# A selective-state mixer whose result is kept with channels on the partitions, its decays read back from DRAM one chunk at a time

## The chip, the cores and the metric
The program runs on one core of a Trainium2 chip. The metric is the device time of one execution in microseconds (us): median of several runs.

## The reference, cut to what matters
Two layers. Layer 0 is a gated state-space mixer and an FFN, both on the same input; layer 1 is attention and a mixture of experts. Only the mixer's part is changed. It works on 2 sequences of 1024 tokens, width 256, with 64 heads of 64 channels in 8 groups (8 heads share one B and one C of 128 states):

```python
proj = einsum('bld,pd->blp', hidden_states, W_in)      # gate, x, B, C, dt
hbc  = silu(conv4(hbc) + conv_b)                       # causal, 4 taps, by channel
dt   = softplus(dt + dt_bias); Abar = dt * -exp(A_log)
scores  = einsum('bclhn,bcshn->bhcls', C_c, B_c)
Y_diag  = einsum('bhcls,bcshp->bclhp', scores * Lmat, x * dt)
states  = einsum('bcshn,bhcs,bcshp->bchpn', B_c, decay_states, x * dt)
Y_off   = einsum('bclhn,bchpn,bhcl->bclhp', C_c, prev_states, exp(A_cs))
Y = Y_diag + Y_off + D * x
g = Y * silu(gate)
out = (g * rsqrt(mean(g*g over the group) + EPS) * norm_weight) @ W_out.T
```

`A_cs` is the running sum of `Abar` inside a chunk, `Lmat` the lower triangle of exp of its differences. The reference cuts chunks of 32 tokens, the kernel of 128; the result does not depend on it.

## The kernel before, in words
The program is a row of stages: `prelude` (layernorm, layer 0's FFN, and the decays for all heads), `mixer`, a short sum, then layer 1. In `mixer` the time goes slot by slot: 128 chunks (8 groups of heads x 2 sequences x 8 chunks of 128 tokens), one slot each, after five slots that only fill. Each engine has its own program, written out in order by `for c in SLOTS`; semaphores tie them together. An engine does its instructions strictly in that order, so where an instruction stands decides what waits behind it. In slot `c`, chunk `c` is prepared, chunk `p = c - 1` is computed, and chunk `e = c - 2` is added to the result.

- **Blocks.** The projection of x, B and C is made in blocks of 128 channels x 384, 388 or 260 tokens, 18 for each group and sequence, so 2 or 3 blocks a slot (nine in four slots). Of each block TensorE does six passes (`fill`, the helper lines L75 to L77) into one of two PSUM banks `pp`; ScalarE starts the convolution (`init`, L966), VectorE adds three taps (`taps`, L1043), ScalarE takes a tanh (`squash`, L972) and VectorE finishes the silu (`finish`, L1050). For the last block of a slot, `squash` and `finish` come first in the next slot.
- **Preparing chunk c.** TensorE transposes x (L911) and B (L917), makes the scores (L918), and the decay exponents of 8 heads in two halves (`decays`, L872) through one PSUM bank `pd`. ScalarE copies x and B out (L993, L996) and takes exp of both halves (L1002, L1007). VectorE multiplies with the scores (L1093, 128x1024). GpSimd makes x times dt (L829), the same with the decay to the chunk's end (L832), and D times x (L834).
- **Computing chunk p, tokens on the partitions.** TensorE: C times the state carried in, 512 channels wide (L883), and 8 products of a head's 128x128 scores as weights with its 64 channels (L890). VectorE scales the first by exp(A_cs) (L1057), GpSimd adds D times x (L822), VectorE adds the two (`y`, L1068). The gate's projection is six passes of 512 columns (helper lines, into `pgt`), ScalarE's tanh (L989), VectorE's silu (L1073) and product (L1076). ScalarE squares and sums over the channels (L1012), GpSimd makes the rsqrt (L844, L846). TensorE transposes `y` (L949), ScalarE copies it out as `gt` (L981), and four products with `wo` (L941) and one VectorE instruction (L1103) add it to the result.
- **The state.** L928 on TensorE, L1085 or L1089 on VectorE, the decay on GpSimd (L839). The first chunk of a sequence has no state carried in, the last makes none.
- **Weights.** SP loads a group's `w_raw` and `wo_raw` two slots into the group before it; GpSimd splits them in nine pieces, one a slot (L799, L809, L812).

A float32 matmul is two passes in the trace (512 columns: L883 x2 in one group); the projections are three passes of rounded parts.

## Time and profile before

| | us |
|---|---|
| median of 3 runs | 2651.09 (2649.43 to 2652.48) |
| the profiled execution, its own time | 2650.09 |
| its span | 2648.4 |
| mixer, of the span | about 242 to 1612 |
| TensorE busy | 2365.0 (89%) |
| VectorE busy | 2069.6 (78%) |
| ScalarE, GpSimd busy | 1169.7, 1157.6 (44% each) |

The page's busy line says how much of the span an engine worked; what limits a stage has to be read in a stretch of that stage. "Idle before" is the time in which an engine stood still ahead of the instructions of a group, with the instruction that ended it. PEclk is the granted TensorE clock, 1.0 for 2.4 GHz.

### The profile page before, as it was taken

The numbers are of one execution on the slowest core, as the hardware profiler recorded it, in microseconds if no ns is written. First come the engines' busy times: TensorE is split into PE (matmuls) and PEld (weight loads), VectorE is DVE, ScalarE is ACT, GpSimd is POOL, SyncE is SP. The second block draws the span as 40 slices with busy tenths as digits, with TensorE's granted clock in tenths as the row PEclk, the third lists the DMA queues.
The fourth block names the chain that finished last, engine by engine and source line by source line (L and its number), as shares of the span: only waits on it lengthen the run. The fifth ranks groups of instructions, "written<-read, shape, count | busy, mean of one in ns | idle before, by whom it ended". The sixth has DMA issues, their size and how long they took to land. (4 is left out here: it accounts for less than half of the span.)

```text
span 2648.4 us, 41294 instructions
## 1 busy us (share of the span) xinstructions
PE 2365.0 (89%) x14084; PEld 1847.5 (70%) x14084; DVE 2069.6 (78%) x3420; ACT 1169.7 (44%) x2311; POOL 1157.6 (44%) x1249
## 2 busy tenths in 40 slices
...
PEclk9996899999999999999999997599999998699996
...
DMA packets 74320, 81.68 MB, mean 31 GB/s; under 512 B 21504, under 2 KB 57696, under 8 KB 72864
## 3 DMA queue, kind: packets, MB, share of 16 engines
...
## 5 line engine op out<-in xcount | busy, mean ns | idle before, releaser
L1043 DVE SCALAR_TENSOR_TENSOR mix_cv<-mix_pp,mix_cw,mix_cv 128x384 f32<-128x384 f32 (+4 forms) x864 | 493.0, 571 | 25.3 <-ACT mix_cv L966 4.5
L890 PEld LDWEIGHTS mix_pyd<-mix_xdt,mix_lm 128*128 128x128 f32 x2048 | 249.1, 193 | 56.7 <-issue 53.1
L966 ACT ACTIVATE mix_cv<-mix_pp,mix_cb,mix_cw 128x384 f32<-128x384 f32 (+1 forms) x288 | 182.1, 632 | 211.5 <-PE mix_pp L77 211.5
L75 PE MATMUL mix_pp<-l0in_XH,mix_wx_lo 128*128 128x384 f32 (+2 forms) x576 | 238.5, 414 | 39.3 <-DVE mix_ss L1032 23.3
L829 POOL TENSOR_TENSOR mix_xdt<-mix_xtok,l_dt 128x512 f32<-128x512 f32 x128 | 133.5, 1043 | 279.2 <-ACT mix_xtok L993 279.2
L1202 POOL TENSOR_TENSOR ffn_hl<-ffn_h,ffn_hh 128x512 fp32r<-128x512 f32 x112 | 144.3, 1288 | 250.5 <-ACT ffn_hh L1260 250.5
L941 PE MATMUL mix_pgt<-mix_wo,mix_gt 128*128 128x256 f32 x1024 | 244.9, 382 | 2.9 <-issue 2.2
L890 PE MATMUL mix_pyd<-mix_xdt,mix_lm 128*128 128x64 f32 x2048 | 244.4, 273 | 2.5 <-DVE mix_lm L1093 2.5
L822 POOL TENSOR_TENSOR mix_t<-mix_t,mix_xd 128x512 f32<-128x512 f32 x112 | 144.4, 1289 | 219.5 <-DVE mix_t L1057 136.9
L1725 DVE TENSOR_REDUCE att_tops<-att_psc 128x1 f32<-128x512 f32 (+3 forms) x384 | 190.0, 550 | 55.5 <-PE att_psc L1673 32.4
L941 PEld LDWEIGHTS mix_pgt<-mix_wo,mix_gt 128*128 128x128 f32 x1024 | 184.1, 190 | 31.2 <-issue 9.2
L972 ACT ACTIVATE mix_pp<-mix_cv 128x384 f32<-128x384 f32 (+1 forms) x288 | 133.0, 462 | 161.6 <-DVE mix_cv L1043 158.3
L1749 ACT ACTIVATE att_pr<-att_pst 128x1024 f32<-128x1024 f32 (+7 forms) x256 | 156.5, 657 | 103.6 <-PE att_pst L1690 73.7
L77 PE MATMUL mix_pp<-l0in_XH,mix_wx_hi 128*128 128x384 f32 (+2 forms) x576 | 188.0, 326 | 0.0
L76 PE MATMUL mix_pp<-l0in_XL,mix_wx_hi 128*128 128x384 f32 (+2 forms) x576 | 187.9, 326 | 0.0
L1276 DVE SCALAR_TENSOR_TENSOR ffn_h<-ffn_th,ffn_pg 128x512 f32<-128x512 f32 x112 | 77.0, 687 | 137.4 <-ACT ffn_th L1255 137.4
L1260 ACT ACTIVATE ffn_hh<-ffn_h 128x512 fp32r<-128x512 f32 x112 | 71.2, 636 | 249.0 <-DVE ffn_h L1283 249.0
L1093 DVE TENSOR_TENSOR mix_lm<-mix_lm,mix_pmisc 128x1024 f32<-128x1024 f32 x128 | 156.1, 1219 | 23.0 <-ACT mix_lm L1007 21.3
L75 PEld LDWEIGHTS mix_pp<-l0in_XH,mix_wx_lo 128*128 128x128 f32 x576 | 111.6, 194 | 88.0 <-DVE mix_cv L1050 38.3
L1068 DVE TENSOR_TENSOR mix_y<-mix_pyd,mix_t 128x512 f32<-128x512 f32 x112 | 77.5, 692 | 111.2 <-POOL mix_t L822 111.2
L1050 DVE SCALAR_TENSOR_TENSOR mix_cv<-mix_pp,mix_cv 128x384 f32<-128x384 f32 (+1 forms) x288 | 145.7, 506 | 9.3 <-ACT mix_pp L972 9.3
L75 PE MATMUL ffn_po<-ffn_dh,ffn_hl 128*128 128x256 f32 x448 | 145.0, 324 | 4.2 <-DVE l_F L1290 4.2
...
## 6 DMA issues: line engine op xcount, KB each, us to landing
...
mix_ll<-cs SPq DMA_DIRECT2D x384, 4.0 KB
mix_wo_raw<-in_w_out SPq DMA_DIRECT2D x8, 512.0 KB, 6.5
...
```

Source lines behind the costliest of these rows:

```text
L75: pe.matmul(out, l_lo, r_hi, start=start, stop=False)
L76: pe.matmul(out, l_hi, r_lo, start=False, stop=False)
L77: return pe.matmul(out, l_hi, r_hi, start=False, stop=stop)
L822: pool.tensor_tensor(t1[p % 2][:, :], t1[p % 2][:, :], xd[p % 2][:, :], ALU.add).then_inc(t1x_done, 1)
L890: last = pe.matmul(pyd[:, h * HP:(h + 1) * HP], lm[p % 2][:, h, :], xdt[p % 2][:, h * HP:(h + 1) * HP], start=True, stop=True)
L941: last = pe.matmul(pgt[:, 0:D], gt[e % 2][:, k * P:(k + 1) * P], wo[:, e // 16 % 2, k, :], start=k == 0, stop=k == NX - 1)
L966: act.activation(conv_tile(k), pp[k % 2][:, halo:cols], ACT.Identity, bias=cb[:, it // 2, ct:ct + 1], scale=cw[:, it // 2, ct, 3:4]).then_ ...
L1043: last = dve.scalar_tensor_tensor(out, of, cw[:, g, ct, 3 - d:4 - d], out, ALU.mult, ALU.add)
L1050: dve.scalar_tensor_tensor(c, pp[k % 2][:, 0:cols - halo], 1.0, c, ALU.add, ALU.mult).then_inc(conv_done, 1)
L1093: dve.tensor_tensor(lm[c % 2][:, :, :], lm[c % 2][:, :, :], pmisc[:, N0:N0 + Q].unsqueeze(1).to_broadcast([P, GH, Q]), ALU.mult).then_inc( ...
L1725: dve.tensor_reduce(tops[o][:, col:col + 1], psc[PLACE[n, g] % RING][:, 0:end - c], AX.X, ALU.max).then_inc(mx_done, 1)
L1749: act.activation(pr[m % 2][:, AT[k]:AT[k + 1]], pst[k % 2][:, 0:1024 - k * P], ACT.Exp).then_inc(ex_done, 1)
```

## The change
The mixer's result is now kept with the channels on the partitions.

- **Off-diagonal and diagonal parts.** For each head one product with the carried state as weights (128x64) and `ce` = C times exp(A_cs) as data (128 columns), and one with x times dt as weights (128x64) and the scores as data, both into the same place in `py` (L918, L920). Even heads write partitions 0 to 63, odd heads 64 to 127. 16 products of 128 columns take the place of one of 512 and eight of 64 columns. The transposes of `y`, their copy, L1057 and L822 are gone.
- **ce.** The table exp(A_cs) goes to DRAM in the prelude (two transfers), laid out by chunk, so that 8 heads x 128 tokens are one run of 4 KB. SP reads it for each chunk to all 128 partitions (512 KB, 112 times, L798), behind a wait for the product that last read the buffer; GpSimd multiplies it with C (128x1024, L842).
- **D times x** is now four 128x128 ScalarE copies with a scale for each channel (L1035).
- **Gate.** Twelve passes of 256 columns for two chunks' tokens and half of the channels, one slot earlier (`gate(c + 1)`), ahead of the second half of the decays. Its tanh (L1026) stands between the two exps on ScalarE; VectorE writes its silu (L1102) to `sg` in SBUF.
- **Sum of squares.** ScalarE squares without a sum (L1008), GpSimd adds four blocks in two instructions (L846, L849), TensorE sums over the partitions with a column of ones (L959); ScalarE copies the sum out (L1002), GpSimd does one power (L838).
- **Order.** On TensorE, `decays(c, 1)` stood behind the slot's last block and now stands ahead of the middle block and the state; the product with `wo` (L964) is done for `p` instead of `e`. On VectorE the addition to the result (L1086) moves from the slot's end to near its start.
- **Loads.** SP loads a group's weights behind waits for the last group's projections and products; `wo` is loaded in place. There is one slot less at the end.

```diff
@@ TensorE
-                        pe.matmul(pyos[:, :], cv[:, CT_C, cols_of(p)], carry[:, :], start=True, stop=True).then_inc(yo_done, 1)
...
-                        for h in range(GH):
-                            last = pe.matmul(pyd[:, h * HP:(h + 1) * HP], lm[p % 2][:, h, :],
-                                             xdt[p % 2][:, h * HP:(h + 1) * HP], start=True, stop=True)
+                        for k in range(NX):
+                            if p % CPS:
+                                for h in (2 * k, 2 * k + 1):
+                                    pe.matmul(head_out(h), carry[:, h * HP:(h + 1) * HP], ce[p % 2][:, h, :], start=True, stop=False)
+                            for h in (2 * k, 2 * k + 1):
+                                last = pe.matmul(head_out(h), xdt[p % 2][:, h * HP:(h + 1) * HP], lm[p % 2][:, h, :],
+                                                 start=p % CPS == 0, stop=True)
...
                         decays(c, 0)
+                    if 0 <= c + 1 < NC:
+                        gate(c + 1)
+                    if live:
+                        decays(c, 1)
                     if len(ks) > 2:
                         fill(ks[1])
...
                         fill(ks[-1])
-                    if live:
-                        decays(c, 1)
...
+                        pe.matmul(px[:, D:D + 1], zs[:, :], one[:, :], start=True, stop=True)
@@ ScalarE
                         act.activation(lm[o][:, 0:4, :].rearrange("p h l -> p (h l)"), pd[:, :], ACT.Exp).then_inc(l_done, 1)
+                    if 0 <= c + 1 < NC:
+                        act.wait_ge(gate_done, c + 2)
+                        wait(act, w_done, c + 1)
+                        act.activation(tg[:, :], pgt[:, :], ACT.Tanh, scale=0.5).then_inc(tg_done, 1)
+                    if live:
+                        act.wait_ge(d_done, 2 * c + 2)
+                        act.activation(lm[o][:, 4:8, :].rearrange("p h l -> p (h l)"), pd[:, :], ACT.Exp).then_inc(l_done, 1)
@@ VectorE
-                        dve.tensor_tensor(by_head(t1[o]), by_head(pyos), heads(TE1, p), ALU.mult).then_inc(t1_done, 1)
                     if len(fills(c - 1)) > 1:
                         finish(fills(c - 1)[-1])
+                    if 0 <= e < NC:
+                        dve.wait_ge(op_done, e + 1)
+                        dve.wait_ge(rs_done, e + 1)
+                        row = ACC[:, e // CPS % 2 * CPS + e % CPS, :]
+                        dve.scalar_tensor_tensor(row, px[:, 0:D], rs[e % 2][:, 0:1], row, ALU.mult, ALU.add).then_inc(acc_done, 1)
...
                     if ks:
                         taps(ks[0])
-                    if 0 <= p < NC:
-                        dve.wait_ge(tg_done, p + 1)
-                        dve.scalar_tensor_tensor(pgt[:, :], tg[:, :], 1.0, pgt[:, :], ALU.add, ALU.mult).then_inc(w_done, 1)
+                    if 0 <= c + 1 < NC:
+                        u = c + 1
+                        dve.wait_ge(tg_done, u + 1)
+                        dve.scalar_tensor_tensor(sg[:, u // 2 % 2, u % 2 * 2:u % 2 * 2 + 2, :].rearrange("p k l -> p (k l)"),
+                                                 tg[:, :], 1.0, pgt[:, :], ALU.add, ALU.mult).then_inc(w_done, 1)
                     if ks:
                         finish(ks[0])
@@ SP
+                    if j:
+                        wait(sp, yd_done, c - 1)
+                        sp.dma_start(ce[c % 2][:, :, :], ecs_d[b * CPS + j, g * GH:(g + 1) * GH, :].partition_broadcast(P)).then_inc(ecs_in[c % 2], 16)
```

ScalarE's program in the middle of the mixer, one slot of two blocks, before:

```order
L981 ACTIVATE mix_gt<-mix_pxt 128x512
L972 ACTIVATE mix_pp<-mix_cv 128x384
L966 ACTIVATE mix_cv<-mix_pp,mix_cb,mix_cw 128x384
L989 ACTIVATE mix_tg<-mix_pgt 128x512
L993 ACTIVATE mix_xtok<-mix_pxt 128x512
L996 ACTIVATE mix_btok<-mix_pmisc 128x128
L972 ACTIVATE mix_pp<-mix_cv 128x384
L1002 ACTIVATE mix_lm<-mix_pd 128x512
L1007 ACTIVATE mix_lm<-mix_pd 128x512
L1012 ACTIVATE mix_junk,mix_ss<-mix_y 128x512
L966 ACTIVATE mix_cv<-mix_pp,mix_cb,mix_cw 128x384
```

and now (L989 is now the tanh of a block, L983 its start, L1026 the gate's tanh):

```order
L989 ACTIVATE mix_pp<-mix_cv 128x384
L1002 ACTIVATE mix_ss<-mix_px,mix_eps_sum 128x1
L983 ACTIVATE mix_cv<-mix_pp,mix_cb,mix_cw 128x384
L1008 ACTIVATE mix_zsq<-mix_z 128x512
L1013 ACTIVATE mix_xtok<-mix_px 128x512
L1016 ACTIVATE mix_btok<-mix_pmisc 128x128
L989 ACTIVATE mix_pp<-mix_cv 128x384
L1022 ACTIVATE mix_lm<-mix_pd 128x512
L1026 ACTIVATE mix_tg<-mix_pgt 128x512
L1029 ACTIVATE mix_lm<-mix_pd 128x512
L1035 ACTIVATE mix_xd<-mix_cv,mix_dsk 128x128 x4
L983 ACTIVATE mix_cv<-mix_pp,mix_cb,mix_cw 128x384
```

The gate's tanh has moved from ahead of the first block's tanh to behind it and behind the first exp.

VectorE's program there, from the finish of the last slot's block on, before:

```order
L1057 TENSOR_TENSOR mix_t<-mix_pyos,l_exp_cs 128x512
L1050 SCALAR_TENSOR_TENSOR mix_cv<-mix_pp,mix_cv 128x384
L1068 TENSOR_TENSOR mix_y<-mix_pyd,mix_t 128x512
L1043 SCALAR_TENSOR_TENSOR mix_cv<-mix_pp,mix_cw,mix_cv 128x384 x3
L1073 SCALAR_TENSOR_TENSOR mix_pgt<-mix_tg,mix_pgt 128x512
L1076 TENSOR_TENSOR mix_y<-mix_y,mix_pgt 128x512
L1050 SCALAR_TENSOR_TENSOR mix_cv<-mix_pp,mix_cv 128x384
```

and now (L1069 the taps, L1076 the finish of a block, L1102 the gate's silu):

```order
L1076 SCALAR_TENSOR_TENSOR mix_cv<-mix_pp,mix_cv 128x384
L1086 SCALAR_TENSOR_TENSOR main_X<-mix_px,mix_rs,main_X 128x256
L1093 TENSOR_TENSOR mix_z<-mix_py,mix_xd 128x512
L1095 TENSOR_TENSOR mix_z<-mix_z,mix_sg 128x512
L1069 SCALAR_TENSOR_TENSOR mix_cv<-mix_pp,mix_cw,mix_cv 128x384 x3
L1102 SCALAR_TENSOR_TENSOR mix_sg<-mix_tg,mix_pgt 128x512
L1076 SCALAR_TENSOR_TENSOR mix_cv<-mix_pp,mix_cv 128x384
L1109 TENSOR_TENSOR mix_lm<-mix_lm,mix_pmisc 128x1024
```

The addition to the result has come between the finish and the chunk's sum, and L1057 is gone.

TensorE's program there, around the slot's start, now (L77 is the block's last pass, L964 the product with `wo`):

```order
L77 MATMUL mix_pp<-l0in_XH,mix_w_hi 128x384
L959 MATMUL mix_px<-mix_one,mix_zs 128x1
L964 MATMUL mix_px<-mix_wo,mix_z 128x256 x4
L918 MATMUL mix_py<-mix_ce,mix_carry 64x128 x2
L920 MATMUL mix_py<-mix_lm,mix_xdt 64x128 x2
```

The pair L918, L920 comes four times. Before, the second half of the decays stood between L77 and the product with `wo`, which the transposes of `y`, the 512 wide L883 and the eight L890 followed.

## Rows read from the trace of the kernel before
**Rows 1.** The page: busy time by engine, and the granted clock in 40 slices.
```profile
PE 2365.0 (89%) x14084; PEld 1847.5 (70%) x14084; DVE 2069.6 (78%) x3420; ACT 1169.7 (44%) x2311; POOL 1157.6 (44%) x1249
...
PEclk9996899999999999999999997599999998699996
```
**Rows 2.** Busy time in one stretch of the mixer, 700 to 1500 us.
```profile
700.00:1500.00 800.00, 787.28 (x4739) 655.64 (x4738) 705.74 (x1204) 444.58 (x955) 476.93 (x537) 1.00 0.04 12
```
**Rows 3.** Groups of VectorE instructions, 700 to 1500 us: xcount | busy us, mean ns | idle before.
```profile
L1043 DVE SCALAR_TENSOR_TENSOR mix_cv<-mix_pp,mix_cw,mix_cv 128x256 f32<-128x256 f32 (+2 forms) x516 | 293.3, 568 | 12.2
L1093 DVE TENSOR_TENSOR mix_lm<-mix_lm,mix_pmisc 128x1024 f32<-128x1024 f32 x77 | 93.9, 1219 | 13.6 <-ACT mix_lm L1007 12.6
...
L1068 DVE TENSOR_TENSOR mix_y<-mix_pyd,mix_t 128x512 f32<-128x512 f32 x66 | 45.7, 692 | 64.5 <-POOL mix_t L822 64.5
L1057 DVE TENSOR_TENSOR mix_t<-mix_pyos,l_exp_cs 128x512 f32<-128x512 f32 x67 | 45.6, 681 | 0.0
```
**Rows 4.** Timeline of the mixer, TensorE: start us, us, engine line op.
```profile
1001.61 1.89 PE L941 MATMUL mix_pgt<-mix_wo,mix_gt 128*128 128x256 f32 x8
...
1003.34 0.60 PE L949 MATMUL mix_pxt<-all_ident,mix_y 128*128 128x128 f32 x4
...
1003.78 1.02 PE L883 MATMUL mix_pyos<-mix_carry,mix_cv 128*128 128x512 f32 x2
...
1004.64 1.89 PE L890 MATMUL mix_pyd<-mix_xdt,mix_lm 128*128 128x64 f32 x16
...
1006.34 0.42 PE L75 MATMUL mix_pp<-l0in_XH,mix_wx_lo 128*128 128x384 f32 x1
...
1009.85 1.02 PE L928 MATMUL mix_pyos<-mix_xdtd,mix_btok 128*128 128x512 f32 x2
...
1011.77 0.39 PE L872 MATMUL mix_pd<-mix_rl,mix_ll 96*128 96x256 bf16 x2
```
**Rows 5.** Timeline of the attention: TensorE, outputs on four partition ranges.
```profile
2402.68 1.05 PE L1705 MATMUL att_po<-att_pr,l_V 128*17 128x512 f32 x8
2403.67 0.39 PE L1673 MATMUL att_psc<-att_ks,att_qs 96*128 96x512 bf16 x1
```
**Rows 6.** Timeline of the mixer: ScalarE and VectorE.
```profile
1007.67 0.67 ACT L966 ACTIVATE mix_cv<-mix_pp,mix_cb,mix_cw 128x384 f32<-128x384 f32 x1 [1.61 <-PE mix_pp L77]
...
1008.53 1.91 DVE L1043 SCALAR_TENSOR_TENSOR mix_cv<-mix_pp,mix_cw,mix_cv 128x383 f32<-128x383 f32 x3
...
1010.47 0.50 ACT L972 ACTIVATE mix_pp<-mix_cv 128x384 f32<-128x384 f32 x1 [0.16 <-DVE mix_cv L1043]
...
1010.90 0.58 ACT L1002 ACTIVATE mix_lm<-mix_pd 128x512 f32<-128x512 f32 x1
...
1016.24 0.68 DVE L1057 TENSOR_TENSOR mix_t<-mix_pyos,l_exp_cs 128x512 f32<-128x512 f32 x1
...
1016.84 0.55 DVE L1050 SCALAR_TENSOR_TENSOR mix_cv<-mix_pp,mix_cv 128x384 f32<-128x384 f32 x1
```
**Rows 7.** Timeline of the mixer's first blocks: VectorE.
```profile
245.01 0.56 DVE L1050 SCALAR_TENSOR_TENSOR mix_cv<-mix_pp,mix_cv 128x384 f32<-128x384 f32 x1 [0.56 <-ACT mix_pp L972]
```
**Rows 8.** Timeline of the mixer's last chunks: VectorE.
```profile
1593.62 1.22 DVE L1093 TENSOR_TENSOR mix_lm<-mix_lm,mix_pmisc 128x1024 f32<-128x1024 f32 x1 [0.21 <-ACT mix_lm L1007]
...
1602.25 1.22 DVE L1093 TENSOR_TENSOR mix_lm<-mix_lm,mix_pmisc 128x1024 f32<-128x1024 f32 x1 [0.21 <-ACT mix_lm L1007]
```
**Rows 9.** Groups of ScalarE instructions, 700 to 1500 us.
```profile
L989 ACT ACTIVATE mix_tg<-mix_pgt 128x512 f32<-128x512 f32 x76 | 45.4, 597 | 57.2 <-PE mix_pgt L77 57.2
...
L1012 ACT ACTIVATION_READ_ACCUMULATOR mix_junk<-mix_y 128x1 f32 x77 | 14.9, 193 | 0.0
```
**Rows 10.** Groups of GpSimd instructions, 700 to 1500 us.
```profile
L846 POOL TENSOR_TENSOR mix_rs<-mix_rs,mix_half 128x1 f32<-128x1 f32 x77 | 42.3, 549 | 6.0
...
L799 POOL TENSOR_TENSOR mix_wo<-mix_wo_raw,mix_nw 128x1024 f32<-128x1024 f32 x5 | 9.5, 1893 | 0.0
```
**Rows 11.** DMA issues: bytes, median us from issue to landing.
```profile
mix_wo_raw<-in_w_out SPq DMA_DIRECT2D x8, 512.0 KB, 6.5
```

335 lines of the change are left out of this document (166 added, 169 removed).

## The prediction
> **What bounds the kernel now.** I read the page first. TensorE is busy for 89% of the span, no other engine for more than 78% [rows 1]. That share is a mean over stages, so I looked at a stretch inside the mixer, the only stage whose work changes: of 800 us TensorE is busy for 787.3 and VectorE for 705.7, and the granted clock is 1.00, the 2.4 GHz level [rows 2]. TensorE paces the mixer; VectorE follows closely.
>
> How long a slot is: the stretch holds 76.5 slots (L1093 appears 77 times [rows 3], its neighbours 76), so a slot is 800 / 76.5 = 10.46 us. VectorE works 705.7 / 76.5 = 9.22 us of it and stands still for 1.23. The groups of VectorE say where: 64.5 us ahead of L1068 (it waits for GpSimd's sum, which ends when VectorE isn't needed yet), 13.6 ahead of L1093, 12.2 ahead of the taps [rows 3]; what is left of the 94.3 us is 4.0. So the slack of VectorE is 1.23 us a slot. A busy engine in second place with that little slack is what decides here: if the change gives VectorE new waits of more than it takes work away, VectorE paces the mixer in TensorE's place.
>
> **The change on TensorE.** From the start of one instruction to the start of the next [rows 4]: L883 0.86 us (1003.78 to 1004.64), the eight L890 1.70, the transposes of `y` 0.44 (four of 128 columns, 0.11 each). The new group is 16 float32 products of 128 columns, thus 32 passes of 0.107: 3.42 us if they go one after the other, 1.71 if the two heads of a pair, on different partitions of the output, go side by side. The trace of before has such a case: L1705 writes four partition ranges, and eight passes of 512 columns, 0.43 each by L883 x2, are followed by the next matmul after 0.99 us [rows 5], not after 3.4. They ran four abreast, with 0.13 us lost at the switch. I take side by side: 1.71 us and two switches, 0.26. The Trainium skill speaks against it: "TensorE: Matmul & The Clock Gate", Part 3, The mechanism, says that a weight load overlaps running matmuls only where the row groups differ, and both heads here use all 128 rows. By that rule this group would come near the 3.42 us; the row of L1705, whose loads also use 128 rows, disagrees. That row has 17 columns of weights and ours 64, so the rule stays as a rival. The sum of squares is two passes of one column behind a full weight load, 0.21 by the transposes' pace. The gate's twelve passes of 256 columns carry as many columns as the six of 512: nothing, or 0.03.
> Net on TensorE: -0.86 - 1.70 - 0.44 + 1.71 + 0.26 + 0.21 + 0.03 = -0.79 us a slot, to some 9.7.
>
> **The change on VectorE, work.** L1057 goes: 0.60 us from its start to the next [rows 6], in 7 of 8 chunks, -0.52. The other instructions keep their sizes: the chunk's sum and product, the gate's silu, L1109, the state, the addition. Reading `sg` from SBUF instead of PSUM I count at nothing. Work: 9.22 - 0.52 = 8.70 us.
>
> **The change on VectorE, waits.** These come from where the instructions now stand, and the order shows them.
> (a) Behind the first block's taps VectorE's next instruction is the gate's silu (L1102). It needs the gate's tanh, which ScalarE does behind the first block's tanh and behind the first exp. The block's tanh needs the taps. So after each first block VectorE stands still for three ScalarE instructions: 0.02 + 0.46 (mean of the forms; 0.50 for 384 columns) - 0.06 + 0.59 - 0.07 + 0.60 + 0.03 = 1.57 us. The steps are rows: taps end at 1010.44, the tanh starts at 1010.47, the exp at 1010.90, 0.07 before the tanh ends [rows 6]; the gate's tanh takes 0.597 [rows 9]. Before, the gate's tanh stood ahead of all this and the silu found it done.
> (b) The last block's taps are followed at once by its finish, which needs ScalarE's tanh. In the first slots, where nothing lies between, this costs 0.56 us each time [rows 7]; 0.51 over the forms. Before, L1057 or the addition filled it.
> (c) The addition to the result has moved behind that finish. It needs GpSimd's power (0.549 [rows 10]), that needs ScalarE's copy of the sum (about 0.19, as the one-column read [rows 9]), and that comes behind the same tanh: 0.19 + 0.08 + 0.55 + 0.03 - 0.06 = 0.79 from the tanh's end, against 0.54 for the finish, so 0.25 more.
> (d) The other small waits, 12.2 + 4.0 us in 76.5 slots, stay: 0.21. The waits for L822 and ahead of L1093 go, since (a) covers them.
> VectorE's round: 8.70 + 1.57 + 0.51 + 0.25 + 0.21 = 11.24 us, against 10.46: +0.78 us a slot. This is a closed ring, as VectorE's own order closes it, and TensorE at 9.7 fits inside.
>
> **Does something else end later?** The ring through TensorE: the second half of the decays needs the first exp, and behind it in order stand the state (0.85), the block (1.07), the sum of squares, the product with `wo` (1.73), the new group and the next first block (1.07), whose taps release the tanh and the exp again. 0.22 + 0.85 + 1.07 + 0.21 + 1.73 + 1.97 + 1.07 = 7.1 on TensorE, then 0.2 to the block's start on ScalarE, 0.67, taps 1.92, and 1.1 for tanh and exp [rows 4, 6]: 11.0 us for two blocks of 384 columns. VectorE's ring over the same blocks is 11.1: the mean of 11.24 has 2.25 blocks of 0.568 x 3 + 0.50 = 2.2 us [rows 3], thus 5.0 us of block work, where two of 384 columns have 1.91 x 2 + 0.55 x 2 = 4.9. So TensorE waits for the exp in every slot and hides inside VectorE's ring with only 0.1 us to spare there; slots of three blocks have more, since the third adds 2.2 us to VectorE's ring and 1.07 to TensorE's.
> GpSimd works 476.9 / 76.5 = 6.2 us of a slot now [rows 2]. It gets L842 (1.9, the size of L799 [rows 10]) and two small sums, and loses L822, D times x and a small addition; even with nothing taken off for these it has 9 us of work in 11, and L842 has most of a slot's time. ScalarE works 444.6 / 76.5 = 5.8 us; it gets four copies of a quarter of L989's size (at most 0.6 each) and loses the transposed copy, and the four stand where it waits for the next block. Neither is on the path; an excess would show as a later xtok and then a later product. SP's transfer for `ce`: 512 KB, 6.5 us to landing for a transfer of that size behind a larger one [rows 11]. SP issues it when the product of two chunks before is done, 12 us before GpSimd's turn, so nothing waits; if that cover were gone, GpSimd and then the next slot's products would wait by the excess. The small decay tables queue behind it for at most those 6.5 us and are needed a slot later. The waits on other groups' weights are over when SP comes to them. The prelude's two transfers are issued while its products still run: nothing. I count `wo` in place at nothing.
>
> **The sum.** 123 slots carry blocks: 123 x 0.78 = +96 us. The last four have none and take 8.63 us now (L1093 at 1593.62 and 1602.25 [rows 8]); without taps only (c) is left there, and TensorE's saving counts: -0.5 each, -2 us. The slot less at the end is empty. Sum: +94 us on the profiled execution, 2650.1 to 2744; the median of the runs is 1 us above that execution, so **2745 us**.
>
> Bounds of this case: with (c) and (d) at nothing the ring is 10.78, +0.32 us a slot, +37 us: 2688. With the products only partly side by side (2.6 us instead of 1.71) TensorE's ring takes over at 11.9 less 0.3 for the shorter forms, or where memory traffic lengthens VectorE's instructions by 4% the ring is about as long: 11.6 to 11.7, +150 us at most: 2800; with both a little more, 2830.
>
> **Rivals.**
> 1. Faster. TensorE goes on to set the pace, as it does now. This needs VectorE's waits to stay below 10.46 - 8.70 = 1.76 us a slot, where I find 2.54; that is the point from which it decides. For it: TensorE was busy for 98.4% of the stretch [rows 2], and the change takes 0.79 us a slot from it. Against it: (a) and (b) alone are 2.08, and both follow from the order, not from estimates. The time: 128 x -0.79 = -101 us, 2550. It would need the gate's tanh to be ready when the taps end.
> 2. Much slower. The head pairs do not run side by side. TensorE's ring then has 3.42 for 1.71 and no switch: 12.4 for 384 columns, about 12.2 over the forms, +1.75 us x 123 = +215: 2866. For it: weights of 64 columns are not 17, and the skill's rule above. Against it: L1705 [rows 5].
> 3. The change does not do what it says: `ce` comes too late, and each slot waits for it. For this 512 KB would have to take 12 us, not 6.5 [rows 11]; priced at +1 to +3 us a slot it gives 2780 to 3030.
>
> **How the numbers follow.** VectorE's ring as told 0.81, rival 1 0.10, rival 2 0.06, rival 3 0.03. The forecast is the first case's. The range 2688 to 2830 is that case's own with its bounds, and leaves out about 2 in 10: the other three and a little of its edges. Within 0.2% (5 us, about what a measurement of this kernel can tell from no change) lies only a ring where the waits happen to cancel, 1.76 us: 0.02. Faster: 0.10. Slower: 0.88.
>
> **What would show it.** In the profile after: a slot of 11.2 us; idle ahead of the gate's silu (L1102) released by ScalarE's gate tanh (L1026), about 1.57 us a time, 190 us in all; idle ahead of the finish (L1076) about 0.5 and ahead of the addition (L1086) about 0.25; TensorE busy for some 87% of the mixer at a clock that stays at 1.00, and waiting at L896 for the exp; the pair L918, L920 in about 2 us for 32 passes. If L1102 finds its tanh done, the forecast is wrong in its main term; if the 32 passes take 3.4 us, rival 2 holds; if GpSimd's L842 waits for a DMA, rival 3.

## The result and the profile after

| | us |
|---|---|
| before, median of 4 runs | 2651.03 (2649.43 to 2652.48) |
| after, median of 4 runs | 2927.73 (2921.61 to 2929.92) |
| ratio | 1.104, interval 1.1025 to 1.106 |
| span of the profiled execution after | 2927.5 |

The change makes the kernel 277 us slower. The direction was forecast; the size was not: 2927.7 lies 98 us above the upper end of the range, 2830. The mixer now lasts from about 242 to about 1898 us.

The stretch of [rows 2], the same 800 us of the kernel after (the columns are those of [rows 2]: TensorE, its weight loads, VectorE, ScalarE, GpSimd, granted clock, DMA share, GB/s):

```profile
700.00:1500.00 800.00, 654.91 (x4916) 550.68 (x4915) 605.10 (x929) 413.79 (x965) 453.15 (x442) 0.93 0.13 45
```

The groups below appear 62 or 63 times, so the stretch holds some 62.4 slots of **12.8 us**, where 11.2 was forecast. VectorE works 605.1 / 62.4 = 9.70 us of a slot and stands still for 3.12; TensorE works 10.50 and no engine is busy for even 82% of the stretch. The granted clock is 0.93, a mean of spells at its two levels, where it was 1.00 before.

VectorE's groups after, same stretch, the answer to [rows 3] (count | busy us, mean ns | idle before):

```profile
L1069 DVE SCALAR_TENSOR_TENSOR mix_cv<-mix_pp,mix_cw,mix_cv 128x256 f32<-128x256 f32 (+4 forms) x421 | 240.1, 570 | 34.1 <-ACT mix_cv L983 22.7
L1095 DVE TENSOR_TENSOR mix_z<-mix_z,mix_sg 128x512 f32<-128x512 f32 x62 | 92.2, 1488 | 2.1
...
L1093 DVE TENSOR_TENSOR mix_z<-mix_py,mix_xd 128x512 f32<-128x512 f32 x63 | 42.9, 681 | 3.8 <-PE mix_py L920 3.7
L1102 DVE SCALAR_TENSOR_TENSOR mix_sg<-mix_tg,mix_pgt 128x512 f32<-128x512 f32 x62 | 42.6, 687 | 94.3 <-ACT mix_tg L1026 94.3
...
L1086 DVE SCALAR_TENSOR_TENSOR main_X<-mix_px,mix_rs,main_X 128x256 f32<-128x256 f32 x63 | 30.4, 483 | 27.1 <-POOL mix_rs L838 27.1
```

The wait that was the main term is there and has its forecast size: 94.3 / 62.4 = 1.51 us a slot ahead of L1102, 1.57 forecast, released by the gate's tanh. But the second row was not in the forecast: the product with `sg`, L1095, takes **1488 ns**, and the sum before it, L1093, of the same size, 681. The small waits (d), forecast at 0.21, are larger too: 34.1 / 62.4 = 0.55 us a slot ahead of the taps, L1069, alone. Then TensorE and GpSimd, groups of the same stretch:

```profile
L896 PE MATMUL mix_pd<-mix_rl,mix_ll 96*128 96x256 bf16 x248 | 53.0, 299 | 123.7 <-ACT mix_lm L1022 123.7
```
```profile
L842 POOL TENSOR_TENSOR mix_ce<-mix_ce,mix_cv 128x1024 f32<-128x1024 f32 x55 | 130.7, 2377 | 0.0
```

TensorE stands still 2.0 us a slot ahead of L896 for the first exp. L842 takes 2.38 us, not 1.9.

One slot of the timeline shows how these hang together. GpSimd and VectorE:

```profile
1009.45 2.38 POOL L842 TENSOR_TENSOR mix_ce<-mix_ce,mix_cv 128x1024 f32<-128x1024 f32 x1
```
```profile
1010.50 0.69 DVE L1093 TENSOR_TENSOR mix_z<-mix_py,mix_xd 128x512 f32<-128x512 f32 x1 [0.44 <-PE mix_py L920]
1011.22 1.15 DVE L1095 TENSOR_TENSOR mix_z<-mix_z,mix_sg 128x512 f32<-128x512 f32 x1
1012.29 1.51 DVE L1069 SCALAR_TENSOR_TENSOR mix_cv<-mix_pp,mix_cw,mix_cv 128x256 f32<-128x256 f32 x3
```

L1093 reads PSUM and SBUF and runs in 0.69 beside L842. L1095 reads two operands from SBUF. It starts while L842 is under way (to 1011.83) and ends at 1012.37, 0.54 after L842's end. The whole mixer shows the same: in all 111 slots in which the two overlap, L1095 ends 0.54 to 0.56 behind L842, whenever it started, and in the 17 slots without such an overlap (most of them slots that prepare a sequence's first chunk, which has no `ce` product) it takes 0.69. So at most some 0.15 of its 0.69 us of work was done while GpSimd's instruction ran. The Trainium skill, "SBUF — State Buffer", section "Who interferes with whom", has this rule: a VectorE instruction with two SBUF inputs contends with a GpSimd instruction that reads SBUF, and whichever starts first holds the shared ports to its end. The trace agrees, and the prediction had not weighed it.

TensorE in the slot before, with the idle time ahead of L896 in brackets, and in the slot after it:

```profile
1003.01 0.39 PE L896 MATMUL mix_pd<-mix_rl,mix_ll 96*128 96x256 bf16 x2 [1.96 <-ACT mix_lm L1022]
...
1004.41 0.42 PE L77 MATMUL mix_pp<-l0in_XH,mix_w_hi 128*128 128x260 f32 x1
...
1005.56 3.00 PE L964 MATMUL mix_px<-mix_wo,mix_z 128*128 128x256 f32 x8
...
1008.48 0.44 PE L918 MATMUL mix_py<-mix_ce,mix_carry 128*64 128x128 f32 x4
...
1010.38 0.39 PE L75 MATMUL mix_pp<-l0in_XH,mix_w_lo 128*128 128x260 f32 x1
...
1010.72 0.28 PE L77 MATMUL mix_pp<-l0in_XH,mix_w_hi 128*128 128x260 f32 x1
...
1014.79 0.39 PE L896 MATMUL mix_pd<-mix_rl,mix_ll 96*128 96x256 bf16 x2 [1.01 <-ACT mix_lm L1022]
...
1016.74 1.97 PE L964 MATMUL mix_px<-mix_wo,mix_z 128*128 128x256 f32 x8
```

and busy time and clock of that stretch:

```profile
996.00:1003.00 7.00, 3.63 (x29) 3.19 (x27) 5.03 (x8) 3.44 (x9) 4.47 (x5) 1.00 0.20 75
1003.00:1008.00 5.00, 4.99 (x19) 4.09 (x20) 4.11 (x7) 3.07 (x8) 3.86 (x4) 0.66 0.02 4
```

In the seven microseconds to 1003 TensorE was busy for 3.63; behind them the granted clock is 0.66 as a mean over 1003 to 1008. A pass of 260 columns takes 0.42 us there, and 0.28 in the next slot; the product with `wo` takes 3.00 us there and 1.97 in the next slot: part of the first is at 1.2 GHz, the second at 2.4. So, as it looks here, the long idle time is paid for a second time, in the work that follows it; run 10 tests this. The group L918, L920 lies from 1008.48 to 1010.38: 32 passes in **1.90 us**, where 1.97 was forecast for passes side by side.

### The profile page after: what moved, and what is told of

Read it like the earlier page. It is cut to its first block and busy times, and to the rows that moved or that the text cites. A ratio compares the mean times of both kernels' runs of the same rounds, so it can differ in the third digit from the quotient of the medians.

```text
span 2927.5 us, 45825 instructions
## 1 busy us (share of the span) xinstructions
PE 2371.3 (81%) x16164; PEld 1864.9 (64%) x16164; DVE 2121.9 (72%) x3308; ACT 1273.2 (43%) x2695; POOL 1275.9 (44%) x1250
## 5 line engine op out<-in xcount | busy, mean ns | idle before, releaser
L1069 DVE SCALAR_TENSOR_TENSOR mix_cv<-mix_pp,mix_cw,mix_cv 128x384 f32<-128x384 f32 (+4 forms) x864 | 492.4, 570 | 70.1 <-ACT mix_cv L983 46.6
L896 PE MATMUL mix_pd<-mix_rl,mix_ll 96*128 96x256 bf16 x512 | 108.8, 297 | 252.4 <-ACT mix_lm L1022 252.4
L75 PE MATMUL mix_pp<-l0in_XH,mix_w_lo 128*128 128x384 f32 (+2 forms) x576 | 272.7, 473 | 33.6 <-DVE mix_ss L1058 23.2
L983 ACT ACTIVATE mix_cv<-mix_pp,mix_cb,mix_cw 128x384 f32<-128x384 f32 (+1 forms) x288 | 181.7, 631 | 266.4 <-PE mix_pp L77 264.4
L989 ACT ACTIVATE mix_pp<-mix_cv 128x384 f32<-128x384 f32 (+1 forms) x288 | 132.1, 459 | 344.3 <-DVE mix_cv L1069 341.5
L964 PE MATMUL mix_px<-mix_wo,mix_z 128*128 128x256 f32 x1024 | 271.4, 411 | 0.0
L842 POOL TENSOR_TENSOR mix_ce<-mix_ce,mix_cv 128x1024 f32<-128x1024 f32 x112 | 266.2, 2377 | 0.0
L1102 DVE SCALAR_TENSOR_TENSOR mix_sg<-mix_tg,mix_pgt 128x512 f32<-128x512 f32 x128 | 88.0, 687 | 196.5 <-ACT mix_tg L1026 196.5
L838 POOL TENSOR_TENSOR mix_rs<-mix_ss,mix_half 128x1 f32<-128x1 f32 x128 | 70.2, 549 | 366.1 <-ACT mix_ss L1002 364.5
L896 PEld LDWEIGHTS mix_pd<-mix_rl,mix_ll 96*128 96x128 bf16 x512 | 40.9, 101 | 279.7 <-ACT mix_lm L1022 278.2
L964 PEld LDWEIGHTS mix_px<-mix_wo,mix_z 128*128 128x128 f32 x1024 | 199.0, 205 | 24.5
L76 PE MATMUL mix_pp<-l0in_XL,mix_w_hi 128*128 128x384 f32 (+2 forms) x576 | 201.9, 351 | 0.0
L77 PE MATMUL mix_pp<-l0in_XH,mix_w_hi 128*128 128x384 f32 (+2 forms) x576 | 201.1, 349 | 0.0
L1076 DVE SCALAR_TENSOR_TENSOR mix_cv<-mix_pp,mix_cv 128x384 f32<-128x384 f32 (+1 forms) x288 | 146.7, 509 | 71.0 <-ACT mix_pp L989 71.0
L920 PE MATMUL mix_py<-mix_lm,mix_xdt 128*64 128x128 f32 x2048 | 191.6, 273 | 1.3 <-DVE mix_lm L1109 1.3
L1095 DVE TENSOR_TENSOR mix_z<-mix_z,mix_sg 128x512 f32<-128x512 f32 x128 | 187.8, 1467 | 4.4
L75 PEld LDWEIGHTS mix_pp<-l0in_XH,mix_w_lo 128*128 128x128 f32 x576 | 125.0, 217 | 100.4 <-issue 50.9
L918 PE MATMUL mix_py<-mix_ce,mix_carry 128*64 128x128 f32 x1792 | 179.8, 279 | 0.0
```

Source lines behind the costliest of these rows:

```text
L75: pe.matmul(out, l_lo, r_hi, start=start, stop=False)
L76: pe.matmul(out, l_hi, r_lo, start=False, stop=False)
L77: return pe.matmul(out, l_hi, r_hi, start=False, stop=stop)
L842: pool.tensor_tensor(ce[o][:, :, :], ce[o][:, :, :], cv[:, CT_C, cols_of(c)].unsqueeze(1).to_broadcast([P, GH, Q]), ALU.mult).then_inc(ce_ ...
L918: pe.matmul(head_out(h), carry[:, h * HP:(h + 1) * HP], ce[p % 2][:, h, :], start=True, stop=False)
L920: last = pe.matmul(head_out(h), xdt[p % 2][:, h * HP:(h + 1) * HP], lm[p % 2][:, h, :], start=p % CPS == 0, stop=True)
```

## The experiments

A ring is a chain of work and waits that closes on itself once a slot; no slot is shorter than the longest ring. The theory behind the first four: the product with `sg`, held up by the `ce` product, and TensorE's clock are the parts that the forecast lacked; the waits (a) to (c) are near their forecast (1.51, 0.54 and 0.43 us a slot). The rivals: the transfers are to blame, or VectorE's wait (a) alone.

**1. The `ce` product behind x times dt on GpSimd.**

```diff
@@ GpSimd, behind the power (L838)
-                    if live and c % CPS:
...
-                        pool.tensor_tensor(ce[o][:, :, :], ce[o][:, :, :],
...
                            pool.tensor_tensor(by_head(xdtd[o]), by_head(xtok[o]), heads(TDTD, c), ALU.mult).then_inc(xdtd_done, 1)
+                    if live and c % CPS:
...
+                        pool.tensor_tensor(ce[o][:, :, :], ce[o][:, :, :],
```

> The changed kernel with one GpSimd instruction moved: the product that makes ce (L842) now stands behind the two products with dt, and no longer runs while VectorE multiplies z by the gate (L1095). Theory (the two share the way to SBUF): L1095 falls from 1.47 us to 0.69, and VectorE's ring is 0.78 us a slot shorter; 2830 us if that ring alone sets the slot, down to 2880 if the ring through TensorE takes over. Rival (L1095 is slow because both of its inputs lie in SBUF): it stays at 1.47 us and the time at 2928.

Measured: 2787.14 us, ratio 1.051 (1.049 to 1.053): 140.6 us less than after the change. The groups and the stretch of this run:

```profile
L1095 DVE TENSOR_TENSOR mix_z<-mix_z,mix_sg 128x512 f32<-128x512 f32 x68 | 47.1, 692 | 2.4
```
```profile
700.00:1500.00 800.00, 671.76 (x5380) 567.44 (x5378) 609.70 (x1023) 456.09 (x1068) 499.02 (x488) 1.00 0.15 51
```

The product is back at 692 ns and the clock at 1.00. The gain is larger than the 98 us expected of the product alone; the half-clock spells went too, and run 10 prices them by themselves at 52 us or more.

**2. The gate's tanh ahead of the first block's tanh on ScalarE**, nothing else.

```diff
@@ ScalarE
+                        act.activation(tg[:, :], pgt[:, :], ACT.Tanh, scale=0.5).then_inc(tg_done, 1)
                     if ks:
                         squash(ks[0])
...
                         act.activation(lm[o][:, 0:4, :].rearrange("p h l -> p (h l)"), pd[:, :], ACT.Exp).then_inc(l_done, 1)
...
-                        act.activation(tg[:, :], pgt[:, :], ACT.Tanh, scale=0.5).then_inc(tg_done, 1)
```

> The changed kernel with the gate's tanh moved on ScalarE ahead of the first block's tanh, where it stood before the change. Theory (VectorE's ring): the idle ahead of the gate's silu, 1.52 us a slot, goes; the ring through TensorE (second half of the decays behind the first exp) is then close to being the longer one: 2740 to 2790 us. Rival (TensorE's ring at the lowered clock sets the slot already): less than 40 us gained, 2890 or more, and the idle turns up ahead of another VectorE instruction.

Measured: 2936.83 us, ratio 1.108 (1.106 to 1.110), 9 us more than after. The expected 2740 to 2790 missed; the rival's number (less than 40 us gained) came true. The wait (a) is down from 94.3 to 14.5 us in the stretch, and the time is not: VectorE's groups of this run say where it went.

```profile
L1109 DVE TENSOR_TENSOR mix_lm<-mix_lm,mix_pmisc 128x1024 f32<-128x1024 f32 x62 | 75.7, 1221 | 60.4 <-ACT mix_lm L1029 60.4
...
L1102 DVE SCALAR_TENSOR_TENSOR mix_sg<-mix_tg,mix_pgt 128x512 f32<-128x512 f32 x62 | 42.6, 688 | 14.5 <-ACT mix_tg L1020 14.2
```

VectorE gets through the silu earlier and waits for the second exp instead; TensorE still waits 125.3 us in the stretch ahead of L896. Another ring was as long. But the long product and the half-clock spells are both still in this run, so run 3 is the cleaner test.

**3. Both moves together**: the two edits above, nothing else.

> Both moves of the two runs before. Theory: VectorE's ring would be 12.85 - 0.78 - 1.52 = 10.55 us, below the 11.0 us reckoned for TensorE's ring; TensorE's rules: 2700 to 2740 us, TensorE idle ahead of L896 still over 1 us a slot, VectorE idle ahead of the taps. Rival (TensorE's ring rules already): 2850 or more.

Measured: 2789.26 us, ratio 1.053 (1.051 to 1.055): the same as with the first alone, where 2700 to 2740 was expected. So the tanh's place is worth nothing while the `ce` product is out of the way as well. VectorE's wait ahead of L1102 fell from 105.2 us in the stretch (run 1) to 33.1, and 57.6 came up ahead of L1109, for the second exp. TensorE waits longer than in run 1 (89.4) for the first exp:

```profile
L896 PE MATMUL mix_pd<-mix_rl,mix_ll 96*128 96x256 bf16 x274 | 53.1, 275 | 106.9 <-ACT mix_lm L1026 106.9
```

**4. The table is not read from the fourth chunk on** (two numbers are read in its place; the `ce` product is then made from what lies in the buffer).

```diff
@@ SP
+                        if c < 3:
                             sp.dma_start(ce[c % 2][:, :, :], ecs_d[b * CPS + j, g * GH:(g + 1) * GH, :].partition_broadcast(P)).then_inc(ecs_in[c % 2], 16)
+                        else:
+                            sp.dma_start(ce[c % 2][:, 0, 0:2], ecs_d[b * CPS + j, g * GH, 0:2].partition_broadcast(P)).then_inc(ecs_in[c % 2], 16)
```

> The changed kernel with the table of decays read only for the first three chunks; for the others SP reads two numbers a partition, so ce and with it the carried state's part is wrong from then on. All waits stay. Theory: the 57 MB cost nothing, 2928 us within 6, L1095 and L842 as long as before. Rival (the transfers get in the way of VectorE, GpSimd or SP): 2900 or less, L842 nearer to 1.9 us and L1095 shorter.

Measured: 2931.84 us, ratio 1.106 (1.104 to 1.108). The DMA share of the stretch falls from 0.13 to 0.03, the product stays at 1475 ns, and the time stays within the 6 us expected (4 us more). The transfers cost nothing.

**5. The chunk's sum stays in PSUM**, so that the product reads one operand there; the `ce` product stays in its place. TensorE's next group, which writes the same place in PSUM, then has to wait for the product instead of the sum.

```diff
@@ VectorE
-                        dve.tensor_tensor(flat(z[p % 2]), py[:, :], flat(xd), ALU.add).then_inc(u_done, 1)
+                        dve.tensor_tensor(py[:, :], py[:, :], flat(xd), ALU.add).then_inc(u_done, 1)
...
-                        dve.tensor_tensor(z[p % 2][:, :, :], z[p % 2][:, :, :],
+                        dve.tensor_tensor(z[p % 2][:, :, :], py[:, :].rearrange("p (k l) -> p k l", k=NX),
@@ TensorE
-                        wait(pe, u_done, p)
+                        wait(pe, z_done, p)
```

> The changed kernel with one tile moved: the chunk's sum is written back to PSUM in place, so that the z product (L1095) reads one operand from PSUM and only sg from SBUF. GpSimd's ce product stays where it is. Theory A (two instructions whose operands all lie in SBUF, one on VectorE and one on GpSimd, hold each other up, which made L1095 1.49 us long and the ce product 2.38): L1095 falls to about 0.7 us, the ce product to about 1.9 to 2.1, the taps come 0.8 us earlier, and the time falls to about 2790, as in the run with the ce product moved. Theory B (the ce product's place on GpSimd delayed something else, a late xtok or xdt, and the long z product was only a symptom): L1095 gets shorter, but the time stays within 1% of 2928. Theory C (any two SBUF accesses of the two engines collide, however many operands): L1095 stays above 1.2 us.

Measured: 2770.26 us, ratio 1.044 (1.042 to 1.046), 157.5 us less than after. VectorE's and GpSimd's groups, the stretch, and one slot:

```profile
L1102 DVE SCALAR_TENSOR_TENSOR mix_sg<-mix_tg,mix_pgt 128x512 f32<-128x512 f32 x70 | 48.2, 689 | 106.5 <-ACT mix_tg L1026 106.5
L1095 DVE TENSOR_TENSOR mix_z<-mix_py,mix_sg 128x512 f32<-128x512 f32 x69 | 47.7, 692 | 2.3
...
L1086 DVE SCALAR_TENSOR_TENSOR main_X<-mix_px,mix_rs,main_X 128x256 f32<-128x256 f32 x70 | 33.9, 484 | 25.0 <-POOL mix_rs L838 25.0
```
```profile
L842 POOL TENSOR_TENSOR mix_ce<-mix_ce,mix_cv 128x1024 f32<-128x1024 f32 x61 | 145.3, 2381 | 0.0
```
```profile
700.00:1500.00 800.00, 676.87 (x5450) 574.07 (x5451) 616.84 (x1035) 460.06 (x1079) 506.42 (x494) 1.00 0.15 51
```
```profile
1018.48 2.37 POOL L842 TENSOR_TENSOR mix_ce<-mix_ce,mix_cv 128x1024 f32<-128x1024 f32 x1
...
1019.74 0.69 DVE L1095 TENSOR_TENSOR mix_z<-mix_py,mix_sg 128x512 f32<-128x512 f32 x1
```

L1095 still lies wholly inside L842, and takes 0.69 us. One operand's place decides: 1488 to 692 ns, with both instructions where they were. That settles theory A for VectorE, and rules out theory B (the time fell by 5%) and C. It was wrong for GpSimd: L842 takes 2381 ns here too, and 2383 in run 1, where it stands elsewhere, so 2.38 us is its own length.

**6. The same in the kernel before**: the gate's silu goes to a tile in SBUF, so that the product with it (L1076 before, 687 ns there) has two SBUF inputs.

```diff
@@ VectorE of the kernel before
-                        dve.scalar_tensor_tensor(pgt[:, :], tg[:, :], 1.0, pgt[:, :], ALU.add, ALU.mult)
+                        dve.scalar_tensor_tensor(sgx[:, :], tg[:, :], 1.0, pgt[:, :], ALU.add, ALU.mult)
...
-                        dve.tensor_tensor(y[o][:, :], y[o][:, :], pgt[:, :], ALU.mult)
+                        dve.tensor_tensor(y[o][:, :], y[o][:, :], sgx[:, :], ALU.mult)
```

> The kernel before with one tile moved: the gate's silu goes to a tile in SBUF, so that the product with it (L1077 here) has all operands in SBUF, as L1095 has after the change; it took 0.68 us with one operand in PSUM. Theory A: it grows where GpSimd works on full tiles at the same time (44% of the time there), so its mean comes to 0.8 to 1.1 us, with single ones near 1.5; VectorE has 1.23 us of slack a slot, so the time rises by at most 10 us (2651 to 2661). Rival: the length comes from something else in the changed kernel; then the product stays at 0.68 to 0.72 and the time at 2651.

Measured: 2694.97 us, ratio 1.0166 (1.0149 to 1.0182). The product and GpSimd's product with the decay in the kernel before, then VectorE's and GpSimd's groups of this run (the lines are one higher than before the edit):

```profile
L1076 DVE TENSOR_TENSOR mix_y<-mix_y,mix_pgt 128x512 f32<-128x512 f32 x76 | 52.2, 687 | 2.6
```
```profile
L832 POOL TENSOR_TENSOR mix_xdtd<-mix_xtok,l_dt_decay 128x512 f32<-128x512 f32 x67 | 69.9, 1043 | 0.0
```
```profile
L1077 DVE TENSOR_TENSOR mix_y<-mix_y,mix_sgx 128x512 f32<-128x512 f32 x74 | 85.1, 1150 | 2.6
...
L1069 DVE TENSOR_TENSOR mix_y<-mix_pyd,mix_t 128x512 f32<-128x512 f32 x64 | 44.3, 692 | 62.4 <-POOL mix_t L823 62.4
```
```profile
L833 POOL TENSOR_TENSOR mix_xdtd<-mix_xtok,l_dt_decay 128x512 f32<-128x512 f32 x64 | 87.0, 1359 | 0.0
```

The product grows from 687 to 1150 ns, as theory A says, and GpSimd's L833 from 1043 to a mean of 1359: a single one takes 1.04 us, or 1.49 where VectorE's product came first. This is the rule in both directions. The time was under-estimated, +44 us and not at most +10: VectorE's 0.84 us of slack a slot is still there ahead of L1069 (62.4 us), a wait that comes before the product and so did not take it up. The taps behind the product come later, and TensorE, idle for 12.7 us of the stretch before, is idle for 32.1. Of the product's 0.46 us a slot, 0.34 (44 us over 128 slots) reached the time. Slack ahead of the work that grows was of little use here.

**7. Both rings opened, the `ce` product late.** From run 3, moved on top: the second half of the decays back behind the slot's last block on TensorE, the second exp ahead of the last block's start and D times x behind it, the product with the scores behind the state on VectorE.

```diff
@@ TensorE
-                    if live:
-                        decays(c, 1)
                     if len(ks) > 2:
                         fill(ks[1])
...
                         fill(ks[-1])
+                    if live:
+                        decays(c, 1)
```

> The changed kernel with the ce product moved behind x times dt and its decayed form on GpSimd, the gate's tanh ahead of the first block's tanh on ScalarE, and beyond that: on TensorE the second half of the decays stands behind the slot's last block again, on ScalarE the second exp directly ahead of the last block's start with D times x behind that, and on VectorE the product with the scores behind the carried state, ahead of the last taps. Theory R (the ring that sets 11.65 us a slot in the run with the ce product moved goes through the wait of the second half of the decays for the first exp): the idle ahead of L896 nearly goes (under 0.3 us a slot from 1.3), the slot falls to 10.2 to 10.5 us and the time to 2600 to 2660. Rival (VectorE's own order is the bound by itself): the slot stays above 11.2 us and the time above 2740.

Measured: 2739.34 us, ratio 1.033 (1.031 to 1.035). Theory R missed. The slot (11.3 us) is the rival's and the time lies at its edge (above 2740), but the reason is not its own. The idle ahead of L896 went (106.9 to 4.7 us in the stretch), but a new one stands elsewhere: 61.9 us ahead of L918, 45.0 of it for the `ce` product, late since run 1's move.

**8. As 7, and the addition to the result ahead of the last block's finish** (ScalarE's copy of the sum ahead of that block's tanh).

```diff
@@ VectorE
+                        dve.scalar_tensor_tensor(row, px[:, 0:D], rs[e % 2][:, 0:1], row, ALU.mult, ALU.add).then_inc(acc_done, 1)
                     if len(fills(c - 1)) > 1:
                         finish(fills(c - 1)[-1])
...
-                        dve.scalar_tensor_tensor(row, px[:, 0:D], rs[e % 2][:, 0:1], row, ALU.mult, ALU.add).then_inc(acc_done, 1)
```

> The run before it, and ScalarE's copy of the sum of squares stands ahead of the last block's tanh, VectorE's addition to the result ahead of its finish. Theory: waits (b) and (c) of the prediction, 0.51 and 0.25 us a slot, are then filled by work that stands there already; if VectorE's round sets the slot by then, it falls by 0.4 to 0.75 us, to 9.7 to 10.0, and the time to 2560 to 2600, below both kernels. Rival: TensorE's round of 9.7 to 9.8 us of work and its own waits set the slot; then it falls by under 0.2 us, the time within 25 us of the run before it. Third way: the addition waits for the product with wo longer than the finish waited for the tanh, and the time rises.

Measured: 2718.05 us, ratio 1.026 (1.024 to 1.027): 21 us less, far above the 2560 to 2600 expected and inside the rival's 25 us. The wait ahead of the finish goes (3.7 us left), the addition waits instead. TensorE's and VectorE's groups:

```profile
L918 PE MATMUL mix_py<-mix_ce,mix_carry 128*64 128x128 f32 x1008 | 106.6, 277 | 71.6 <-POOL mix_ce L855 54.4 <-DVE mix_lm L1120 17.2
```
```profile
L1084 DVE SCALAR_TENSOR_TENSOR main_X<-mix_px,mix_rs,main_X 128x256 f32<-128x256 f32 x73 | 35.1, 481 | 89.1 <-POOL mix_rs L838 89.1
```

Most of both points at one cause, which run 9 tests: the `ce` product, 2.37 us here, stands late on GpSimd, and the power behind it.

**9. As 8, with the sum in PSUM (run 5) and the `ce` product back in its first place.** The edit is that of run 5 in place of that of run 1:

```diff
@@ GpSimd, behind the power again
+                        pool.tensor_tensor(ce[o][:, :, :], ce[o][:, :, :],
@@ VectorE
+                        dve.tensor_tensor(py[:, :], py[:, :], flat(xd), ALU.add).then_inc(u_done, 1)
```

> The order of e8_reordered_acc_first, with the chunk's sum in PSUM as in e5_sum_in_psum, so that the ce product can go back to its first place on GpSimd at no cost for VectorE. In e8 TensorE stood still 1.0 us a slot ahead of the group L918, 54.4 of 71.6 us of it for the ce product, and the addition waited 1.24 us a slot for GpSimd's power, which stood behind the ce product. Theory (these two waits are what the late place of the ce product costs): both fall below 0.4 us a slot, the slot from 11.1 to 10.2 to 10.4 us, the time to 2600 to 2650, below or at the kernel before. Rival: VectorE's round (8.9 us of work and its waits for the exps) sets the slot at 10.8 or more, and the time stays above 2680.

Measured: **2605.83 us**, ratio 0.983 (0.982 to 0.984), 1.7% faster than the kernel before and inside the 2600 to 2650 expected. The stretch:

```profile
700.00:1500.00 800.00, 758.80 (x6135) 644.05 (x6135) 698.37 (x1166) 508.19 (x1215) 559.54 (x549) 1.00 0.17 57
```

The stretch holds 78.5 slots of 10.2 us; TensorE works 758.8 / 78.5 = 9.67 us of each. The wait ahead of L918 is down from 71.6 to 27.6 us, none of it for the `ce` product, and that of the addition from 89.1 to 2.1.

**10. The kernel after, with more work for TensorE.** The gate's twelve passes are done twice, ahead of the place where TensorE waits.

```diff
@@ TensorE, gate
-                    for t in range(2):
+                    for t in (0, 1, 0, 1):
```

> The changed kernel, with the gate's twelve passes done twice over (the second time onto the same values, so the result is the same): 1.4 us more work for TensorE in each slot at full clock, put in the place where it stands still for 2.0 us a slot ahead of L896. Theory K (the half-clock spells are a cost of their own, brought on by that idle time): TensorE does not stand still long enough for its clock to fall, the granted clock of the stretch 700 to 1500 comes back to 1.00 and the time falls by 20 to 60 us, to 2870 to 2905, in spite of more work. Rival L (the half-clock spells only fill idle time and cost nothing): the time stays at 2928 or rises, by up to 50 us, as the gate's tanh comes 1.4 us later.

Measured: 2875.32 us, ratio 1.085 (1.083 to 1.086): 52 us **less** than after, with 1.4 us more work in every slot (twelve passes that start 0.12 us apart), as theory K said. Its stretch, L896, and VectorE's taps:

```profile
700.00:1500.00 800.00, 723.38 (x5853) 627.85 (x5853) 628.35 (x966) 429.81 (x1008) 468.59 (x457) 1.00 0.14 49
```
```profile
L896 PE MATMUL mix_pd<-mix_rl,mix_ll 96*128 96x256 bf16 x258 | 50.0, 275 | 47.1 <-ACT mix_lm L1022 46.6
```
```profile
L1069 DVE SCALAR_TENSOR_TENSOR mix_cv<-mix_pp,mix_cw,mix_cv 128x256 f32<-128x256 f32 (+4 forms) x441 | 250.8, 569 | 11.7
```

The clock is 1.00 throughout the stretch, and L1095 is as long as ever (1545 ns). So the half-clock spells cost at least 52 us of the 277, and the idle time ahead of L896 brought them on: filled, it is 0.7 us a slot and they are gone. Most of the 52 us can be placed: VectorE's wait ahead of the taps, for a block that TensorE had done late, falls from 0.55 to 0.18 us a slot (11.7 us in 64.5 slots), which over 123 slots is 45 us.

**11. As 5, with TensorE's ring alone opened** (the moves of run 7 on TensorE, ScalarE and VectorE, with the gate's tanh left late and the addition left behind the finish). The edit on TensorE is that of run 7; on VectorE:

```diff
@@ VectorE, behind the finish of the first block
-                        dve.tensor_tensor(lm[c % 2][:, :, :], lm[c % 2][:, :, :],
...
+                        dve.tensor_tensor(lm[c % 2][:, :, :], lm[c % 2][:, :, :],
...
                     if len(ks) > 1:
                         taps(ks[-1])
```

> The run with the sum in PSUM (2770), with TensorE's second half of the decays back behind the slot's last block and the second exp and the product with the scores moved along with it, but with the gate's tanh left behind the block's tanh and the first exp, and with the addition left behind the last block's finish. Moving the gate's tanh alone (with the ce product late) gave nothing. Theory 2R (two rings of nearly one length: VectorE's own with the waits (a) to (c), and the one through TensorE's wait for the first exp; a cut in one alone gives nothing): VectorE's ring is untouched, the idle ahead of L1102 stays near 1.5 us a slot, the slot stays at 11.2 to 11.5 us and the time at 2735 to 2775, though TensorE's idle ahead of L896 falls below 0.4 us a slot. Rival (only TensorE's ring bound that run): the slot falls to 10.3 to 10.7 and the time to 2640 to 2690.

Measured: 2766.98 us, ratio 1.044 (1.042 to 1.046), the same as run 5 and as expected (the median of three executions; a fourth took 4597.72 us and is left out). VectorE's and TensorE's groups:

```profile
L1102 DVE SCALAR_TENSOR_TENSOR mix_sg<-mix_tg,mix_pgt 128x512 f32<-128x512 f32 x69 | 47.5, 688 | 107.5 <-ACT mix_tg L1026 107.5
```
```profile
L896 PE MATMUL mix_pd<-mix_rl,mix_ll 96*128 96x256 bf16 x278 | 54.8, 278 | 4.0 <-ACT mix_lm L1022 4.0
```

TensorE's wait for the exp fell from 92.4 to 4.0 us, and nothing came of it. Together with run 3 this shows two rings of nearly one length: opening VectorE's alone gives nothing (with the `ce` product late), and opening TensorE's alone gives nothing (with the sum in PSUM). Run 9, with both, is 164 us below run 5. Not all of the 164 need be theirs: run 9 also has the addition ahead of the finish, which was worth 21 us in run 8, and no run has the two openings without it.

**12. As 9, with the first exp ahead of the gate's tanh on ScalarE.**

```diff
@@ ScalarE
+                        act.activation(lm[o][:, 0:4, :].rearrange("p h l -> p (h l)"), pd[:, :], ACT.Exp).then_inc(l_done, 1)
...
                         act.activation(tg[:, :], pgt[:, :], ACT.Tanh, scale=0.5).then_inc(tg_done, 1)
                     if ks:
                         squash(ks[0])
...
-                        act.activation(lm[o][:, 0:4, :].rearrange("p h l -> p (h l)"), pd[:, :], ACT.Exp).then_inc(l_done, 1)
```

> The version at 2606, with the first exp ahead of the gate's tanh on ScalarE, where ScalarE waits 0.34 us a slot for the gate's projection. Left there: 0.54 us a slot ahead of L1102, 0.32 ahead of the product with the scores (L1120), 0.35 ahead of L918 for that product. Theory (the second half of the decays, and so the second exp and the product with the scores, come too late because the first exp is late): the first exp is done 0.6 to 1.1 us earlier, the idle ahead of L896 goes, and the slot falls by 0.05 to 0.3 us, to 2565 to 2600. Rival: the exp takes 0.59 us where only 0.34 are free, so the gate's tanh and all behind it come 0.25 us later, and the slot grows by as much: 2606 to 2640.

Measured: **2585.51 us**, ratio 0.9755 (0.9742 to 0.9769), the fastest version of this study, inside the 2565 to 2600 expected. TensorE no longer waits ahead of L896, and the product with the scores waits 14.0 us in the stretch where it waited 25.3; the gate's silu waits a little longer, 50.0 for 42.4.

## Why the prediction was right in part, and where it failed

- **The failed step** is one sentence of VectorE's work: "Reading `sg` from SBUF instead of PSUM I count at nothing". L1095 took 1488 ns instead of 692, since GpSimd's product, which reads SBUF, ran beside it; runs 1, 5 and 6 show it in both kernels, put in and taken out. The order of the change showed L1095 with both inputs in SBUF, and GpSimd's full-width L842 beside it was counted only as time of GpSimd, never as something that VectorE could meet.
- **The second failed step** is the clock that "stays at 1.00". It did so in runs 1, 3, 5, 8, 9, 10 and 12 (0.99 in 7 and 11), not in the kernel after: 0.93. The product's 0.8 us stands ahead of the first block's taps, so the exp comes later, and TensorE's wait ahead of L896 is 2.0 us a slot where run 5 has 1.3. Runs 1 and 5, which only free the product, have it back at 1.00, so the second failure follows from the first.
- **The account.** Run 5 is the change without these two: 2770. The forecast was 2745. Its slot is 800 / 69.8 = 11.46 us, forecast 11.24: work 8.84 for 8.70; (a) 1.53 for 1.57; (b) 0.53 for 0.51; (c) 0.36 for 0.25; (d) 0.21 for 0.21. That is +0.22 x 123 = 27 us, and 2745 + 27 = 2772. So VectorE's ring without the product was sized well, term by term and not by luck. From run 5 to run 10, which has the long product at full clock, are 105 us; over the whole run L1095 is busy for 196.6 us there and for 88.6 in run 5, 108 more, so its growth fell on the time almost in full. From run 10 to the kernel after are another 52. (That 2770 + 105 + 52 gives 2927 is no test of its own, since the steps are differences of measured times; the 27 and the 108 are.)
- **TensorE's work, -0.79 to some 9.7**: the level is right, the saving less so. Run 9 has 9.67 at a clock of 1.00. But 9.7 was reached from the slot, 10.46; TensorE was busy for 787.3 / 76.5 = 10.29 of it before, so busy time fell by 0.62, not 0.79. The 32 passes took 1.90 us, where 32 of 0.107 would be 3.42, so the two heads of a pair do run side by side. With that rival 2 falls. The sentence that it drew on, in the Trainium skill, "TensorE: Matmul & The Clock Gate", Part 3, The mechanism, lets a weight load overlap running matmuls only where the row groups differ. The trace disagrees: these loads use all rows, and the passes still lie abreast.
- **TensorE's ring** that "hides inside VectorE's ring with only 0.1 us to spare" was rightly found, and its closeness was the real warning: runs 3 and 11 show both rings at nearly one length. A term that lies in both, as the product with `sg` does, then falls on the time in full. Its length, 11.0 us, was too short: run 3, with VectorE's wait (a) cut to a third, still has a slot of some 11.7. Which term is short is not shown.
- **L842** was counted at 1.9 us by L799; it took 2.38. In run 5 that costs nothing. In the kernel after, where L1095 ends 0.55 behind it, its extra 0.48 us is by estimate over half of what L1095 grew by; in runs 7 and 8, where it stood late, TensorE and the addition waited for it.
- **Rival 1** (faster) fell: the waits were 3.12 us a slot, and 2.62 in run 5; its limit was 1.76. **Rival 3** fell too: `ce` landed in 3.7 us, and run 4 shows that its transfers cost nothing.
- **The range** bounded terms that the prediction had named. Longer VectorE instructions were among them, but only as 4% of the work, some 0.35 us a slot, through memory traffic; the product alone grew by 0.80, and not through the transfers (run 4). The clock had no bound. The two together are worth 157 us, where the range reaches 85 above the forecast.

What stays open: the 52 us is a lower bound, since run 10 also has more work; what TensorE's doubled passes cost by themselves no run shows. And in run 12 VectorE is still idle for 800 - 707.1 = 92.9 us of the stretch, 50.0 of them ahead of the gate's silu; whether another order on ScalarE would gain from that was not tried.
